# Bias copies of a mixture-of-experts kernel by GpSimd, between its scatters, and one slot fewer

## The reference

```python
x = x + attention_block(layernorm(x))      # 16 heads, causal mask with relative biases, MLP of 512
x = x + ffn(layernorm(x))
x = x + recurrence(layernorm(x))           # gated scan along the sequence, then a layernorm
x = x + ffn(layernorm(x))

def ffn(x, router_w, gate_w, gate_b, up_w, up_b, down_w, down_b):   # 8 experts, top 2
    xf = x.reshape(b * s, d)                                        # 8192 tokens of 128
    probs = jax.nn.softmax(xf @ router_w.T, axis=-1)
    topv, topi = jax.lax.top_k(probs, 2)
    mask = jnp.zeros_like(probs).at[jnp.arange(n)[:, None], topi].set(1.0)
    probs = probs * mask
    probs = probs / (probs.sum(axis=-1, keepdims=True) + 1e-09)
    g = jnp.einsum('nd,edf->nef', xf, gate_w) + gate_b              # 256 hidden units
    u = jnp.einsum('nd,edf->nef', xf, up_w) + up_b
    h = jax.nn.silu(g) * u
    expert_out = jnp.einsum('nef,efd->ned', h, down_w) + down_b
    return jnp.einsum('ne,ned->nd', probs, expert_out)
```

## Time and profile before

| | us |
|---|---|
| median of 3 runs | 1616.85 |
| lowest and highest run | 1606.71, 1619.03 |
| the profiled execution, span from its first to its last instruction | 1782.9 |
| attention phase (to about 926, tables and start included) | 926 |
| first expert stage | 926 to 1190 |
| recurrence phase | 1190 to 1468 |
| second expert stage | 1468 to 1735 |
| combine | 1735 to 1783 |

### The profile page before, as it was taken

The page is one execution under the profiler, slowest core; times in us unless marked ns, Lnnn a source line. Parts: engine busy times, 40 slices in busy tenths (PEclk is TensorE's granted clock), DMA queues, the critical chain, the costliest instruction groups (busy, mean ns, idle before and its releaser), DMA issues. The chain is left out here.

```text
span 1782.9 us, 37607 instructions
## 1 busy us (share of the span) xinstructions
PE 1384.4 (78%) x11633; PEld 1127.5 (63%) x11633; DVE 1254.2 (70%) x3903; ACT 783.3 (44%) x1754; POOL 957.3 (54%) x1156
## 2 busy tenths in 40 slices
PE   3699999999899999998628888746776718878860
PEld 2467777777677777776528778745555518877850
DVE  4478998888889878875356556538888845555647
ACT  1134555454445444544115444426666624444520
POOL 2214556666656666653645555543777764555550
PEclk8568999998999989996659898978878858889885
DMA  7101111111111111110322222211222122222218
GB/s 212 44 34 40 40 45 47 52 52 47 45 49 47 47 52 41 51 46 8 111 79 70 80 76 76 78 58 48 73 74 74 58 64 76 78 75 77 77 53 283
DMA packets 101873, 121.99 MB, mean 68 GB/s; under 512 B 18168, under 2 KB 81712, under 8 KB 101424
## 3 DMA queue, kind: packets, MB, share of 16 engines
q1 hardware_dynamic: 72592, 77.73, 14.5%
q0 software_dynamic: 17408, 36.21, 6.0%
q10 hardware_dynamic: 11680, 5.66, 1.2%
HBM read 49.72 MB, written 44.72 MB: 53 GB/s over the span
## 5 line engine op out<-in xcount | busy, mean ns | idle before, releaser
L1020 DVE TENSOR_REDUCE mx<-max_banks 128x6 f32<-128x768 f32 x256 | 243.0, 949 | 70.2 <-PE max_banks L769 50.3
L1049 DVE TENSOR_TENSOR ebuf<-score_banks,region 128x768 f32<-128x768 f32 x256 | 243.0, 949 | 33.0 <-PE score_banks L795 30.1
L1277 ACT ACTIVATE region<-ebuf 128x768 f32<-128x768 f32 x256 | 216.3, 846 | 99.6 <-DVE ebuf L1049 97.1
L1669 POOL DMA_INDIRECT choice_rows<-second_yo,second_xg x144 | 139.0, 965 | 130.6 <-DVE second_yo L1789 95.3
L1669 POOL DMA_INDIRECT choice_rows<-first_yo,first_xg x144 | 138.8, 964 | 128.3 <-DVE first_yo L1789 93.2
L2079 POOL DMA_INDIRECT expert_rows<-d_rows,z_d_index x128 | 130.2, 1017 | 38.7 <-issue 32.0
L1546 POOL DMA_INDIRECT expert_rows<-d_rows,a_d_index x128 | 128.3, 1003 | 36.9 <-issue 32.1
L757 PE MATMUL max_banks<-identb,region 128*128 128x128 bf16 x512 | 109.0, 235 | 35.3 <-DVE mx L1020 26.0
L1437 POOL TENSOR_TENSOR rs<-arg,neghalf 128x4 f32<-128x4 f32 x32 | 33.1, 1035 | 181.3 <-DVE arg L997 181.3
L814 PE MATMUL bankO<-region,vaug 128*32 128x256 f32 (+1 forms) x2048 | 126.8, 356 | 2.5 <-ACT region L1277 1.6
L1745 ACT ACTIVATE second_silu<-second_bgu,second_biases 128x256 f32<-128x256 f32 x144 | 64.0, 477 | 133.0 <-issue 56.1
(11 more groups left out here) (329 smaller groups left out, 4349.6 us busy)
## 6 DMA issues: line engine op xcount, KB each, us to landing
region_r<-region_r SPq DMA_DIRECT2D x192, 128.0 KB
first_xg<-expert_rows SPq DMA_DIRECT2D x72, 132.0 KB
second_xg<-expert_rows SPq DMA_DIRECT2D x72, 132.0 KB
z_rows<-choice_rows SPq DMA_DIRECT2D x32, 256.0 KB
c_rows<-choice_rows SPq DMA_DIRECT2D x16, 512.0 KB
out<-xres ACTq DMA_DIRECT2D x16, 256.0 KB
choice_rows<-first_yo,first_xg POOLq DMA_INDIRECT x144
choice_rows<-second_yo,second_xg POOLq DMA_INDIRECT x144
```

The lines of the kernel that those rows point to most:

```text
L1020: nc.vector.reduce_max(mx[:, n, places:places + 5:4, :], max_banks[:, :, 0:BK].rearrange("p h (k c) -> p h k c", k=3), AXX).then_inc(maxed ...
L1049: nc.vector.tensor_tensor(ebuf[:, half_of_ebuf(c, j), :, :], score_banks[:, :, 0:BK], bias32[:, plain(j), :], ALU.add).then_inc(scores_fre ...
L1277: nc.scalar.activation(p32[:, j % 4, :, :], ebuf[:, half_of_ebuf(c, j), :, :], ACT.Exp).then_inc(exped, 1)
L1669: pool.indirect_dma_start(choice_dram, bass.IndirectOffsetOnAxis(ap=xg[:, i % G, t, E:E + 1].bitcast(I32), axis=0), yo[:, i % 4, t, :], No ...
```

## The change

In the expert stage GpSimd now copies the biases, half a slot's (2 of 4 values per partition) behind each scatter: behind the two scatters of slot i stand the copies for slot i+6. The copies of slots 0 to 5 are made ahead of the loop. The ring `biases` has eight places in place of four, and the copy waits for `hid_done` of the slot eight before its own. GpSimd loads the expert words as the other engines do. VectorE's copy and its wait go. The stage runs over `s.TURNS` = 71 slots; the tables keep their 72 entries (`s.SLOTS`), and SP's last waits count the scatters of each of the four semaphores.

```diff
-        self.SLOTS = -(-(2 * self.N // self.Q + self.NE - 1) // self.BODY) * self.BODY
+        self.TURNS = 2 * self.N // self.Q + self.NE - 1
+        self.SLOTS = -(-self.TURNS // self.BODY) * self.BODY
...
 def run_dispatched(nc, s, tag, ident, w, slots_dram, choice_dram):
-    NE, EF, E, ST = s.NE, s.EF, s.E, s.SLOTS
+    NE, EF, E, ST = s.NE, s.EF, s.E, s.TURNS
...
-        biases = sb("biases", [P, 4, 2 * NF])
+        biases = sb("biases", [P, 8, 2 * NF])
...
             @block.gpsimd
             def _(pool):
+                AHEAD = 6
+
+                def bias(j, e, k):
+                    if j >= 8 and k == 0:
+                        pool.wait_ge(hid_done, (j - 7) * NF)
+                    return nc.gpsimd.tensor_copy(biases[:, j % 8, k * NF:(k + 1) * NF],
+                                                 w["bias"][:, bass.ds(e, 1), k * NF:(k + 1) * NF].rearrange("p a f -> p (a f)"))
+
+                for j in range(AHEAD):
+                    if j % 4 == 0:
+                        e = experts_around(pool, j)
+                    bias(j, e(j), 0)
+                    bias(j, e(j), 1).then_inc(b_ready, 1)
                 for i in range(ST):
+                    j = i + AHEAD
+                    if j % 4 == 0 and j < ST:
+                        e = experts_around(pool, j)
                     pool.wait_ge(y_done, i + 1)
                     for t in range(2):
                         pool.indirect_dma_start(
                             choice_dram, bass.IndirectOffsetOnAxis(ap=xg[:, i % G, t, E:E + 1].bitcast(I32), axis=0),
                             yo[:, i % 4, t, :], None,
                         ).then_inc(stored[i % 4], 16)
+                        if j < ST:
+                            half = bias(j, e(j), t)
+                            if t == 1:
+                                half.then_inc(b_ready, 1)
...
-                                             bias=biases[:, i % 4, f:f + 1]).then_inc(silu_done, 1)
+                                             bias=biases[:, i % 8, f:f + 1]).then_inc(silu_done, 1)
...
                 def low(i, e):
-                    if i >= 4:
-                        dve.wait_ge(hid_done, i * NF + (NF - 4 * NF))
-                    nc.vector.tensor_copy(biases[:, i % 4, :], w["bias"][:, bass.ds(e, 1), :].rearrange("p a f -> p (a f)")
-                                          ).then_inc(b_ready, 1)
-
...
-                                                       biases[:, i % 4, NF + f:NF + f + 1], act_[:, f, :], ALU.add, ALU.mult
+                                                       biases[:, i % 8, NF + f:NF + f + 1], act_[:, f, :], ALU.add, ALU.mult
...
                 for q in range(4):
-                    sp.wait_ge(stored[q], 32 * ST // 4)
+                    sp.wait_ge(stored[q], 32 * len(range(q, ST, 4)))
```

More of the change, by code:

```diff
@@ L1630, in run_dispatched @@
     expert = w["expert"]
-    assert ST % 8 == 0 and NE == 8 and NF == 2
+    assert NE == 8 and NF == 2
     with phase(nc) as (ctx, new_sem):
```

## The result

The changed kernel takes 1632.73 us (median of 18 runs) where the kernel before takes 1619.09 in the same sessions: a ratio of 1.0079, 95% interval 1.0054 to 1.0104, some 13 us more. The forecast was 1654, 37 more. The direction is right and the size is wrong: the loss is a third of what was forecast.

A forecast was written before the change was run, and what follows sets the result against it. The prediction took GpSimd, level with TensorE before, to become the expert stages' bound at 2.90 us a slot: 71 x 2.90 instead of 72 x 2.6 adds 18.7 us a stage, so 1616.85 + 37 = 1654 us, range 1604 to 1695.

The forecast's parts named there:

- What bounds: Expert stages: TensorE at 2.55 and GpSimd at 2.52 us a slot are level; a timed slot lasts about 2.6.
- VectorE's part: Expert stages: removing VectorE's bias copy and wait, 12.7 us of work a stage, was counted as 0 gain.
- GpSimd's part: Between expert-stage scatters: a copy C of 0.17 makes the period 1.28 + C = 1.45 us, 2.90 a slot.
- The register operations: On GpSimd: computing each copy's address costs nothing; if not hidden, 0.40 us a slot.
- 71 slots: Expert stages: dropping the last slot saves one period, about 2.6 to 2.9 us a stage, and two scatters.
- The sum: Expert stages: 71 x 2.90 replaces 72 x 2.6, 18.7 us more a stage, 37 in two.
- The way back: Expert stages: GpSimd's lag stays hidden until four slots, some 10 us, then VectorE waits ahead of yo.
- The port rule: A two-port VectorE copy or cast and a GpSimd operation exclude each other, so new copies can stand behind the weight cast.
- rival (a): Copies on GpSimd each stand for half a VectorE cast, 0.21 us: 48.5 us more a stage, 1714 us; chance 0.10.
- (b): Halts or something else stretch timed expert slots to 2.9 or more, so GpSimd has room: 1610 to 1611 us; chance 0.20.
- (c): VectorE's chain in the expert stages sets restart and much of the pace: 30 us go, 1587 us; chance 0.10.
- (d): The copy hides in the 0.30 us between scatters, none late: GpSimd 2.52 to 2.6 a slot, 1612 us; chance 0.12.

The follow-up runs named there:

- e1: The kernel before, unedited, profiled again on the slow chip with halts: its 29 runs took 1767.69 to 1796.85 us.
- e9: The kernel before, unedited, profiled on a chip without halts: median 1615.39 us over 29 runs.
- e3: The changed kernel with one GpSimd copy of all four biases behind a slot's second scatter, on the chip with halts: ratio 0.994 to the kernel before.
- e4: The kernel before with 71 slots and no bias copy on any engine, biases read straight from the table, on the chip with halts: ratio 0.9972.
- e12: The kernel before with 71 slots and no bias copy on any engine, biases read straight from the table, without halts: ratio 0.9967.
- e15: The kernel before with 71 slots, VectorE copying, plus a 128x2 GpSimd TENSOR_SCALAR with a constant behind each scatter: 1662.33 us.
- e16: The kernel before with 71 slots, VectorE copying, plus a 128x2 GpSimd TENSOR_SCALAR with two per-partition operands behind each scatter: 1727.12 us.
- e14: The kernel before with 71 slots, VectorE copying, plus a 128x2 GpSimd cast at a fixed address behind each scatter: 1628.4 us.
- e10: The kernel before with 71 slots alone, VectorE still copying, without halts: 1604.55 us against 1615.39, ratio 0.9955.
- e13: The kernel before with 71 slots, VectorE copying, plus a 128x2 GpSimd memset behind each scatter: 1607.86 us, ratio 0.9959.
- e11: The changed kernel with one GpSimd copy of all four biases behind a slot's second scatter, without halts: ratio 1.0034 to the kernel before.

## Why the prediction was right and wrong

**What bounds.** Right in what it concluded: TensorE's 2.55 and GpSimd's 2.52 us a slot are level, and more work on GpSimd makes it the bound. It took the 166 us between profile and runs for time that no timed run has, without a cause. They are in every run on one chip (e1) and in none on the chips of the result. The slot of "about 2.6 us" was near: e9 shows 2.54 for TensorE and 2 x 1.277 = 2.55 by the scatters. Which of the two engines set the 2.55 before was not tried. On the chip of e1 the argument probably fails, since one copy a slot cost nothing there (e3).

**VectorE's part** at nothing: right (e4, e12). Its wait for hid_done and its 12.7 us a stage had 0.5 us of cover in each slot.

**GpSimd's part** is the step that failed: "1.28 + C", 1.45 us a scatter. Its terms, as forecast and as the row of the changed kernel shows: gap before the copy 0.02, measured 0.00; copy 0.17, measured 0.19; gap behind it 0.17, measured 0.16; scatter 1.09, measured 0.97. The sum is 1.33 for the usual scatter and not 1.45, and the error of 0.12 is that of the last term. It was read behind a TENSOR_SCALAR with two operands per partition, and e15 and e16 show that this form lengthens the scatter, while a copy, cast or memset whose result the scatter doesn't use leaves it within 0.01 of the 0.96 behind a scatter. In the mean over the stage, with the copies that took longer, a scatter came every 1.356 us, 0.08 more than the 1.277 of before and not the 0.19 of the forecast.

**The register operations** at nothing: right. On GpSimd the ALU_OPs take 35 ns each and lie under the scatters; the cast of e14 has a fixed address and its distance is 1.32 all the same.

**71 slots**: 5 us expected, 0.45% = 7 us measured with an interval of 3 to 12 (e10). Right. Without it the change would have lost about 20 us.

**The sum.** Forecast 71 x 2.90 - 72 x 2.6 = 18.7 us a stage. With the measured sizes it is 142 x 1.356 - 144 x 1.277 = 8.7. The scatter's price takes 142 x 0.12 = 17.0 off. The base of 2.55 instead of 2.6 puts 3.3 on, and the mean distance, 0.026 above the usual one, another 3.7. The second stage lost 5.9. That the direction came out right owes something to the wrong term: with 0.97 in its place and the base left at 2.6, the sum would have been 142 x 1.33 - 187.2 = 1.7 us a stage, too little to tell from no change.

**The way back.** The prediction had the lag grow to four slots, some 10 us, and come back by VectorE's wait ahead of yo, with an undisturbed slot of 2.9. None of this was seen. In the changed kernel's trace the first scatter of a slot starts at most 4.7 us after its yo is written (median 3.2, where e9 has 1.0), no yo waits for a DMA, and the undisturbed slot is 2.55. The waits of TensorE that a DMA ends, the one at 992.81 among them, are for the load of the rows, which the prediction named second. The end of the sum, that the last scatter pays the lag in full, doesn't depend on it.

**The port rule.** The copies' own time and the scatters' distance have a tail. Half of the copies took 183 to 194 ns, but the longest 486, and the mean distance of scatters is 0.03 us above the median's (1.356 and 1.327), while it is 0.01 with the memset, which reads nothing (e13: (1082.9 - 902.1) / 141 = 1.282 against 1.272), and 0.01 before, without any operation (e9: 1.277 against 1.263). VectorE's weight cast has a longer tail too: its mean in the first stage went from 426 to 444 ns while the median stayed (421 and 419). So rival (a), half a cast for each copy, 0.21 us, is refuted: the excess is 0.03 at most, of which some 0.01 was there before. The Trainium skill, page "SBUF — State Buffer", section "Who interferes with whom", has GpSimd and a two-port copy or cast of VectorE lock each other out of their ports; a tail of this kind agrees with that rule, at a seventh or less of the price that I gave it, but no run here moved the cast out of the copies' way, so its cause wasn't tried.

**The rivals.** (b) has its mechanism on the chip with the halts (e3: no loss from one copy a slot there) and not on those of the result. (c) fell with e12. (d), the copy hidden in the 0.30 us, was nearer to the truth than the forecast in this: two thirds of the copy are hidden there (0.19 long, 0.064 more distance), and all of a memset.

## What to carry to other kernels

When an engine is level with the bound to a few hundredths of a microsecond per turn, whatever new work adds to its period is paid in every turn. What it adds has to be read between neighbours of the same form: the price of a scatter depended on the operation ahead of it. Between two indirect scatters of GpSimd lie 0.30 us in which a memset is free, a small copy costs 0.06 to 0.08, and a TENSOR_SCALAR 0.2 to 0.4. The better edit here was to leave the copies where an engine had half a microsecond to spare per slot, and to drop the slot (e10).

## What the runs showed of the hardware

- One of four chips ran the same program 10% slower than the others in all 29 runs of its session (median 1780.55 against 1615.39), with seven to nine slots of over 6 us in each expert stage where the others had none. The medians of TensorE's transposes (272 ns) and products are the same on both chips. In the first stage of e1 the slots of over 6 us are those numbered 12, 19, 28, 35, 44, 48, 55 and 64 from 0, and 12 and 19 are long in its second stage and in both stages of the first profile too, so they may belong to places in the program. What halts it stays open; a profile and the runs that it is compared with should be from the same session.
- A GpSimd copy, cast or memset starts within 0.01 us of the end of the scatter ahead, a TENSOR_SCALAR after 0.04 to 0.05, but a scatter starts 0.16 to 0.19 us after any of them and 0.30 us after a scatter.
- The form of an operation changes how long the scatter behind it takes: 0.96 to 0.97 us behind a copy, cast or memset of 128x2, 1.02 behind a TENSOR_SCALAR with a constant, 1.06 with two per-partition operands. It is 0.98 behind a copy of 128x4 (e11), and 1.05 to 1.11 behind line 244's cast, whose result the scatter sends (e9). Why was not tried.
- Two copies in a row start 0.12 us apart though each is shown with 0.19.
